# Plain heads: a projection's last third split behind later row maxima, and the V product of the first tiles moved behind the fifth maximum

## The reference

```
qk = x @ W_qk + b_qk            # q and k of all heads, 64 each
v  = (x @ W_v + b_v)            # 8 heads of 64
sim  = einsum('bihd,bjhd->bhij', q, k) * scale
attn = softmax(sim, axis=-1)
o    = einsum('bhij,bjhd->bihd', attn, v)
y    = layernorm(o @ W_out + b_out) * gamma + beta
```

## Time and profile before

| what | value |
|---|---|
| three runs | 2705.14, 2707.29, 7025.78 us; median 2707.29 |
| the profiled execution | 2705.34 us, of it a span of 2703.6 us from the first to the last instruction |
| busy share of the span | PE 97%, DVE 60%, POOL 56%, ACT 48% |
| mean granted TensorE clock | 0.990 of full speed |
| attention pass | from the start to about 1905 us, 64 heads |
| a plain head | 25.87 us (25.7 in place 1) |
| a head in place 0 | 37.4 us |

### The profile page before, as it was taken

The page is one execution under the profiler, slowest core; times in us unless marked ns, Lnnn a source line. Parts: engine busy times, 40 slices in busy tenths (PEclk is TensorE's granted clock), DMA queues, the critical chain, the costliest instruction groups (busy, mean ns, idle before and its releaser), DMA issues. The chain is left out here.

```text
span 2703.6 us, 31999 instructions
## 1 busy us (share of the span) xinstructions
PE 2619.8 (97%) x11376; PEld 1792.9 (66%) x11376; DVE 1630.6 (60%) x2679; ACT 1300.5 (48%) x1833; POOL 1521.1 (56%) x819
## 2 busy tenths in 40 slices
PE   7999999999999999999999999999579999999999
PEld 5665656666565666656666666665368888888887
DVE  6555465455545555554554565455377878788785
ACT  3355346345534534543453454354355555555554
POOL 3576577567657756765775676577423333333333
PEclk9999999999999999999999999999789999999999
DMA  3221122122112212211221221122412222222220
GB/s 97 63 52 48 36 79 55 40 71 55 44 40 75 56 40 71 56 43 47 71 53 40 71 60 40 40 52 79 147 67 105 81 105 81 100 83 95 90 78 32
DMA packets 108410, 178.32 MB, mean 66 GB/s; under 512 B 22401, under 2 KB 22913, under 8 KB 108289
## 3 DMA queue, kind: packets, MB, share of 16 engines
q1 hardware_dynamic: 108288, 176.75, 22.8%
HBM read 92.02 MB, written 50.59 MB: 53 GB/s over the span
## 5 line engine op out<-in xcount | busy, mean ns | idle before, releaser
L324 POOL TENSOR_TENSOR acc<-acc,probs 128x1024 f32<-128x1024 f32 x384 | 914.1, 2380 | 356.7 <-ACT probs L623 332.0
L418 DVE TENSOR_REDUCE half_max<-ps_max 128x1 f32<-128x512 f32 x1024 | 684.7, 686 | 409.4 <-PE ps_max L782 401.0
L623 ACT ACTIVATE probs<-ps_st 128x1024 f32<-128x1024 f32 x512 | 521.9, 1023 | 746.7 <-PE ps_st L803 744.4
L814 PE MATMUL ps_o<-probs,v 128*64 128x512 f32 x2048 | 467.7, 598 | 0.0
L802 PE MATMUL ps_st<-qA,kA 128*128 128x512 f32 x1024 | 413.0, 403 | 5.0 <-DMA qB<-max_row 2.4
L782 PE MATMUL ps_max<-kA,qA 128*128 128x512 f32 x1024 | 399.3, 414 | 11.1 <-DVE kA L404 7.6
L803 PE MATMUL ps_st<-qB,kB 65*128 65x512 f32 x1024 | 405.5, 396 | 0.0
L814 PEld LDWEIGHTS ps_o<-probs,v 128*64 128x64 f32 x2048 | 135.7, 136 | 261.8 <-issue 246.2
L782 PEld LDWEIGHTS ps_max<-kA,qA 128*128 128x128 f32 x1024 | 187.9, 188 | 139.8 <-issue 43.3
L802 PEld LDWEIGHTS ps_st<-qA,kA 128*128 128x128 f32 x1024 | 193.5, 189 | 90.5 <-DVE qB L406 26.8
L320 POOL TENSOR_TENSOR acc<-probs 128x1024 f32<-128x1024 f32 x64 | 153.2, 2394 | 159.0 <-ACT probs L623 158.8
(11 more groups left out here) (174 smaller groups left out, 4552.8 us busy)
## 6 DMA issues: line engine op xcount, KB each, us to landing
stage<-in_L_attn_x_dram SPq DMA_DIRECT2D x32, 512.0 KB, 6.0
qA<-qA SPq DMA_DIRECT2D x128, 128.0 KB, 2.3
kB<-kA SPq DMA_DIRECT2D x128, 128.0 KB, 2.4
o_hi_scratch<-spare SPq DMA_DIRECT2D x128, 128.0 KB, 2.3
o_lo_scratch<-oT SPq DMA_DIRECT2D x128, 128.0 KB, 2.4
o_hi<-o_hi_scratch SPq DMA_DIRECT2D x16, 1024.0 KB, 5.5
o_lo<-o_lo_scratch SPq DMA_DIRECT2D x16, 1024.0 KB, 7.7
xc<-in_L_attn_x_dram SPq DMA_DIRECT2D x16, 1024.0 KB, 5.2
```

Source lines behind the costliest of these rows:

```text
L324: pool.tensor_tensor(acc[:, :], acc[:, :], probs[:, j, :], ALU.add).then_inc(acc_done, 1)
L418: dve.tensor_reduce(half_max[:, r, kh:kh + 1], ps_max[(j + 1) % 2][:, :], AX_X, ALU.max).then_inc(max_done, 1)
L623: act.activation(probs[:, j, :], ps_st[j % 2][:, :], ACT.Exp).then_inc(exp_done, 1)
L814: ins = pe.matmul(ps_o[half * DH:(half + 1) * DH, :], v[:, j, hd * DH:(hd + 1) * DH], probs[:, j, half * HALF:(half + 1) * HALF], start=(j ...
```

## The change

Four edits, all of them in the order of calls; no instruction is added or left out.

1. TensorE, `plain_head`: the shared `front` now ends after maximum product 1. What followed it is kept for `late_v_head` as `late_front`, in the old order. Plain heads get `plain_front`: projection 8 and 9, product 2, scores 2, product 3, projection 10 and 11, scores 3.
2. TensorE, `plain_head`: scores 4 before product 4; then the V product of tiles 0 to 3; then products 5 and 6, scores 5, and the rest with the later products closer together.
3. ACT, `plain_head` (which serves place 0 as well) and `scaling_head`: exponents 0 to 2 before `store_qk_hi` of the second half, in place of 0 and 1.
4. DVE, `plain_head`: maxima 0 to 3 before the inverse and `store_qk_lo` of the second half, in place of 0 to 2.

```diff
@@ DVE, plain_head
-                    reduce_max(b, h + 1, 0, 3)
+                    reduce_max(b, h + 1, 0, 4)
                     if h >= 1:
                         invert_sums(b, h - 1)
                     store_qk_lo(b, h + 1, 1)
-                    reduce_max(b, h + 1, 3, 16)
+                    reduce_max(b, h + 1, 4, 16)
                     join_max(b, h + 1)
@@ ACT, plain_head
-                    exponent(b, h, 0, 2)
+                    exponent(b, h, 0, 3)
                     if more:
                         store_qk_hi(b, h + 1, 1)
-                    exponent(b, h, 2, TT)
+                    exponent(b, h, 3, TT)
@@ ACT, scaling_head
-                    exponent(b, h, 0, 2)
+                    exponent(b, h, 0, 3)
                     store_qk_hi(b, h + 1, 1)
-                    exponent(b, h, 2, 4)
+                    exponent(b, h, 3, 4)
@@ TensorE
                     scores(b, h, 1, 2)
                     project_qk(b, h + 1, 1, 4, 8)
                     rows(b, h + 1, 1, 2)
+
+                def late_front(b, h):
+                    front(b, h)
                     project_qk(b, h + 1, 1, 8, 12)
                     rows(b, h + 1, 2, 3)
                     scores(b, h, 2, 3)
                     ...
+                def plain_front(b, h):
+                    front(b, h)
+                    project_qk(b, h + 1, 1, 8, 10)
+                    rows(b, h + 1, 2, 3)
+                    scores(b, h, 2, 3)
+                    rows(b, h + 1, 3, 4)
+                    project_qk(b, h + 1, 1, 10, 12)
+                    scores(b, h, 3, 4)
+
                 def plain_head(b, h, last):
-                    front(b, h)
+                    plain_front(b, h)
                     scores(b, h, 4, 5)
-                    rows(b, h + 1, 5, 6)
+                    rows(b, h + 1, 4, 5)
+                    p_at_v(b, h, 0)
+                    rows(b, h + 1, 5, 7)
+                    scores(b, h, 5, 6)
                     more = not (last and h == HEADS - 2)
+                    rows(b, h + 1, 7, 8)
                     if more:
                         free_of_qk(b, h + 1, 1)
                         project_qk(b, h + 2, 0, 0, 2)
-                    rows(b, h + 1, 6, 7)
+                    rows(b, h + 1, 8, 9)
                     if more:
                         project_qk(b, h + 2, 0, 2, 4)
-                    rows(b, h + 1, 7, 8)
-                    scores(b, h, 5, 6)
-                    rows(b, h + 1, 8, 10)
-                    p_at_v(b, h, 0)
-                    rows(b, h + 1, 10, 12)
+                    rows(b, h + 1, 9, 10)
                     scores(b, h, 6, 7)
-                    rows(b, h + 1, 12, 13)
+                    rows(b, h + 1, 10, 11)
                     if more:
-                        project_qk(b, h + 2, 0, 4, 6)
-                    rows(b, h + 1, 13, 14)
+                        project_qk(b, h + 2, 0, 4, 5)
+                    rows(b, h + 1, 11, 12)
+                    if more:
+                        project_qk(b, h + 2, 0, 5, 6)
+                    rows(b, h + 1, 12, 14)
                     if more:
                         project_qk(b, h + 2, 0, 6, 8)
                     rows(b, h + 1, 14, 15)
@@ late_v_head
-                    front(b, h)
+                    late_front(b, h)
                     free_of_qk(b, h + 1, 1)
```

## The result

The changed kernel takes 2790.43 us (median of 4 runs, 2789.92 to 2791.99) against 2707.25 before: a ratio of 1.0313, 95% interval 1.0296 to 1.0329. The ratio leaves out one run of the kernel before, of 7025.78 us, which nothing here explains. The changed kernel is slower by 3.1%, where 2.5% was forecast (2776, range 2760 to 2796). The profiled execution took 2791.99 us, of it a span of 2790.2; that is 86.7 more than the profiled execution before.

What follows compares the result with a forecast made beforehand. TensorE, busy 97%, was taken to bound the kernel: matmuls times their step, plus losses between them. 52.0 + 1.6 + 16.6 = 70.2 us on 2705.3 gave 2775.5, with half the difference to the median 2776; range 2760 to 2796.

Steps and rivals of the forecast that it cites:

- The rest of k in plain heads: Product 4 in plain heads: ACT's later copies make its load late, a loss of 0.88 us a head.
- The floor of 0.65: Product 4 in plain heads: with the copy right behind the projection, 0.65 us lost, which no ACT order can beat.
- The wait of product 5: Plain heads: its wait for a maximum behind DVE's two subtractions goes, a gain of 0.2 us a head.
- The maxima closer together: Late in plain heads: products 12 and 13 wait for maxima, 0.35 and 0.46, sum 0.81 us a head.
- the near miss: Product 14 in plain heads: its load is free 0.13 us late, which was put at no loss.
- Place 0: Its eight heads: ACT's shared order delays copy and product 4 by 2.08 us, all passed on, + 16.6 us.
- the low clock as a rival: New waits halve the clock for some six matmuls in 49 heads, 59 us more, 2834; chance 0.04.
- the 1.6 forecast: The last plain head has no projection to space its products and loses about 1.6 us.
- The maxima keep pace: Rival, plain heads: products are served sooner, the 0.81 falls away and only waits for k come, 2743; chance 0.06.
- Place 0 hides its copy: Rival, place 0: the delayed copy costs nothing there, 53 us more in all, 2759; chance 0.05.
- Not slower: Rival, decided at product 4's load: old waits go and none replace them, -16 us, 2690; chance 0.05.
- if the granted clock leaves 1.00: Sign in the changed profile: a granted clock other than 1.00 would show the forecast wrong.

Runs made afterwards that it cites:

- sixth experiment: The changed kernel with ACT's order of before in all heads (copies behind exponent 1, exponent 2 behind the copies): 2817.76 us, ratio 1.0411.
- seventh experiment: The kernel before with DVE's new order alone in plain heads (maximum 3 ahead of the inverse and subtractions): 2736.51 us, ratio 1.0110.
- 8: The kernel before, plain heads alone: V product directly behind scores 3, ahead of product 4, later products in pairs: 2722.06 us, ratio 1.0064.
- 9: As 8, with the V product directly behind scores 3 in place 0 too, against the kernel before: 2714.71 us, ratio 1.0029.
- 10: As 9, but in plain heads the twelve products behind the V product three steps apart throughout: 2684.17 us, ratio 0.9919 to the kernel before.
- experiment 4: The changed kernel with nine additional unused matmuls in place 0, in the wait ahead of product 4: 2779.57 us, ratio 1.0275.
- experiment 1: The changed kernel with ACT's order of before in place 0 alone: 2761.08 us, ratio 1.0202.
- 5: The changed kernel with four additional unused matmuls in place 0, in the wait ahead of product 4: 2785.57 us, ratio 1.0291.
- experiment 3: The changed kernel with the V product and all that follows product 4 on TensorE in the order of before: 2785.01 us, ratio 1.0285.
- 2: The kernel before with ACT's new order in place 0 alone (three exponents ahead of the copies): 2734.50 us, ratio 1.0103.

## Why the prediction was right, and where it was short

**What bounds the kernel: right.** TensorE's step of 0.233 is unchanged in the plain heads, and the 86.7 us are all time between matmuls or slower matmuls. The heads that the change doesn't touch on any engine, places 6 and 7, have none of it.

**The rest of k in plain heads: right, a little short.** Forecast 0.88, measured 1.00: from the last matmul of scores 4 (624.22) to the V product's first (625.78) there are 1.56, where two steps and the change of kind (0.09) are 0.56. The difference is ACT's take-up: the copy started 1.05 behind the exponent and not 0.92. The row with 0.92 was one in which ACT went on to a copy of another shape. The floor of 0.65 that "no order of ACT can beat" was given only for product 4 and was not reached: in the sixth experiment, with the copies right behind the projection, scores 4 wait first and lose 1.7, and product 4 behind them has nothing left to wait for.

**The wait of product 5: right.** It is gone in the changed kernel. The seventh experiment shows the price of DVE's edit where nothing covers it: 0.73 a head.

**The maxima closer together: right, a little long.** Forecast 0.81 at products 12 and 13; in the trace projection 6 comes 1.42 behind projection 5 (634.11 to 635.53), where three steps are 0.70: 0.72. Product 14, the near miss that the rule put at nothing, waits 0.15 in 27 of the 40 heads and indeed delays no matmul. That the sum a head fits so well is in part luck, since the two errors nearly cancel: 1.72 - 0.39 = 1.33 a head, and 54.0 / 40 = 1.35 measured. Pairs (8, 9) and even distances (10), with the same twelve products, show that their distance makes the waits.

**Place 0: the wait right, the clock behind it missed.** This is the term that was mis-sized: 16.6 forecast, 30.8 measured. The wait itself came out at 17.7 (experiment 4), again by ACT's take-up. The other 13.1 are the clock. The prediction had the low clock as a rival with 0.04, argued from a head with 1.08 of idle time in one piece that held 1.00, and priced it at some six slow matmuls in each of 49 heads. It came in the eight heads of place 0, with five to eleven matmuls of 0.63 in each, and for three matmuls at the end of the last plain head. The step of the argument that failed is "all is passed on: 8 x 2.08": a wait of 2.08 in place 0 was priced as time alone, although the row that I read for the clock spoke of half that idle time. The kernel before had no row that would have said so: its wait of 2.42 in the first head, longer still, left the clock at 1.00 (experiment 1). The Trainium skill (TensorE: Matmul & The Clock Gate, the section on psum-queue depth-cycling) says of another kernel that frequent short idles between groups of matmuls, while it cycled through PSUM banks, made the clock swing. The plain heads here come nearest to that and don't show it: their 0.75 of idle time came 40 times without a fall behind it. Place 0 is another case, one wait of 2.13 in every eighth head.

**The sum.** 70.2 forecast, 86.7 measured in the profiled executions. Of the 16.5 between, 13.1 are the clock in place 0, 1.1 the wait there, 2.0 the plain heads and 0.3 the last one. The last one's waits alone came out under the 1.6 forecast: it lasts 26.75 in experiments 4 and 5, 1.4 more than before, and 27.26 in the changed kernel, where three of its matmuls are slow. Without the clock the kernel would stand near 2777, so the terms were sized well. That the measured 2790 is inside the range all the same is luck: the range was built from the bounds of the waits and the maxima, with nothing in it for the clock, and the clock took up the room that they left. By its own sign, "if the granted clock leaves 1.00", the forecast is wrong in place 0; of its other signs, the head of 27.2 (27.22) and the load idle for 1.2 (1.18) held, the head of 39.5 in place 0 did not (41.2, and 39.7 with the wait filled).

**The rivals.** *The maxima keep pace* falls with the trace and experiment 3. The row quoted for it, DVE idle for 2.96, lies beside the V product and not early in the head, so it gave the rival no support. *Place 0 hides its copy* falls with experiments 1 and 2. *Not slower* failed at product 4, as argued. *The clock* came true in part, in place 0 and not in the plain heads for which it was priced. What stays open is why idle time of 1.08 to 2.42 us brings the low clock in one head and not in the next: with the same idle time, to the hundredth, both outcomes stand side by side, and no run here tells what decides.

## What to carry to other kernels

When a step is moved behind another to give a wait more cover, follow the chain that ends the wait on every engine: here four steps of cover were bought and the copy at the head of the chain was delayed by more than seven, and a shared function carried the delay into heads with no cover at all. A piece of work that needs nothing late belongs in the wait itself, ahead of the waiting instruction; moving it behind leaves it queued. A consumer that takes 0.70 us an item wants its items 0.70 apart: the same number of steps in pairs costs time at every second pair. And a trace in which a long wait left the clock alone does not say that the next one will: price a wait of one to two and a half us with and without the fall.

## What the runs showed of the hardware

- TensorE's clock fell to the lower of its two levels after 2.13 us of idle time in all eight heads of place 0, after 1.20 in five of eight, after 1.43 in 16 of 40, after 1.08 in none of seven in the kernel before, the changed one and four experiments, and in one to three of seven in six others; after 0.75, forty times in one kernel, never. Yet after 2.42 us in the first head it fell in eight of thirteen traces only. So no single length of idle time parts the two outcomes between 1.08 and 2.42. In these heads a fall cost 1.4 us or more, with steps of 0.43 for 0.233.
- Filling the idle time with matmuls that nothing uses made the kernel faster by 11 us, though it added 72 of them.
- An ACT copy of 64x512 behind an exponent of 128x1024 starts 1.05 after it, a copy of 8x128 0.92.
- The matmul behind a waiting one starts 0.33 after the late weight load: 596.49 and 596.82 in the earlier trace rows, 629.89 and 630.22 in experiment 6. So a wait costs the time from the start of the matmul ahead of it to the load, less 0.13 (two steps of 0.233 less 0.33).
